# First four heads' rows stored and loaded ahead of the rest, in a two-layer transformer kernel on one Trainium2 core

## The chip, the cores and the metric

The program runs on one core of a Trainium2 chip. The core has five engines that run side by side and meet at semaphores: PE (TensorE, matmuls into PSUM), DVE (VectorE), ACT (ScalarE), POOL (GpSimd) and SP (SyncE), which here only issues DMAs. Sixteen DMA engines move the data. The metric is device time in microseconds, lower is better.

## The reference, cut to what matters

```python
# x is (4, 512, 128): B=4, T=512, C=128; H=16 heads of Dh=8
def _L0_attn_ref(x, W_qkv, b_qkv, W_out, b_out):
    qkv = (x @ W_qkv + b_qkv).reshape(B, T, 3, H, Dh).transpose(2, 0, 3, 1, 4)
    q, k, v = (qkv[0], qkv[1], qkv[2])
    ...
    q = q * cos + rotate_half(q) * sin
    k = k * cos + rotate_half(k) * sin
    attn = softmax(einsum('bhqd,bhkd->bhqk', q, k) / sqrt(Dh))
    out = einsum('bhqk,bhkd->bhqd', attn, v)
    return out.transpose(0, 2, 1, 3).reshape(B, T, C) @ W_out + b_out
...
x = _layernorm(x + _L0_attn_ref(x, ...))
x = _layernorm(x + _L0_ffn_ref(x, ...))      # 16 experts, top 4
x = _layernorm(x + _L1_attn_ref(x, ...))     # linear attention
x = _layernorm(x + _L1_ffn_ref(x, ...))      # linear layer with gated low-rank parts
```

## The kernel before

The kernel goes through the four batches of 512 tokens with everything resident in SBUF. The first 230 us are softmax attention of layer 0, and the rest is the expert layer and layer 1.

A head has only 8 dimensions, so one head's product q·k would use 8 of PE's 128 rows. Instead each float32 value is split into three bfloat16 parts (split_done0 counts the parts of k, split_done1 those of q), and all nine products of parts are summed in one bfloat16 matmul over 72 rows: 3 x 3 parts x 8 dimensions. These rows, the **stack**, are built by a trip through DRAM. `store_part` (L328) writes one part of one of the two, 128 rows of 512 tokens, three times over into `stack_dram[b, i]`, whose shape is 72 rows x 16 heads x 512 tokens (i is 0 for k and 1 for q). `load_stack` (L336) reads the 72 rows of four heads back, into `KS` or `QS`. `parts_st0` and `parts_st1` count the stores that landed, 16 for each DMA.

For each of 16 groups G (4 batches x 4 groups of four heads), PE first computes the scores only to find their row maxima (`scores_for_max`, L528; 16 matmuls for each group), and DVE reduces each to `negmax` (L1136). DVE then splits the 16 columns of maxima in parts (`split_max`, the CAST at L1145 is its first step, and `maxq_done` its end). PE transposes them (`max`, L663), ACT copies them to `maxp`, and SP writes them with `load_max` (L349) as three further rows of QS. Only then `scores` (L544) computes the transposed scores with the maximum already taken off, ACT takes the exponential (L837) and `values` (L553) multiplies with v. The maxima run 26 to 36 matmuls ahead of the exponentials.

At the start the order is written by hand. PE: 11 matmuls on zeros (`keep_warm`, L746), four rotary projections of batch 0 (L653), the values (L658), two projections of batch 1 (L653), 42 matmuls on zeros, and then the loop over the first 17 maxima with one matmul on zeros behind each. Behind it come 12 more on zeros, the transposition of the maxima, and nine more maxima, with the first four `scores` among them. DVE rotates batch 0 (L1268) and splits the third part; ACT splits the first two (L946). POOL sets zeros and then rotates and splits batch 1: k's half (seven operations) and q's half (seven operations), by `rope_split` and `rest_split`, and in `rope_split` it waits until the parts of batch 0 are stored, because it writes the same tile. SP issues all DMAs from one queue in program order, and a wait holds all that stand behind it.

Of the kernel before, what the change touches and what calls it, by code (L numbers as in the profile page):

```python
# [67 lines left out]
EARLY = dict(w_kq=4 * D, b_rope=4, cos=T, sin=T, w_v=D, ident=P, bv_row=D)  # L68
# [12 lines left out]

EARLY_AT, EARLY_N = columns(EARLY)
# [5 lines left out]
def program(nc, x_in, xT_in, early_in, late_in, identb_in, ones_in, stack_dram, w_dram, out):  # L88
    with ExitStack() as ctx:
# [9 lines left out]
        c_.update({k: late[:, a:b] for k, (a, b) in LATE_AT.items()})  # L99
        ident = c_["ident"]  # L100
# [67 lines left out]
        split_done = [sem(f"split_done{i}") for i in range(2)]  # L168
        parts_st = [sem(f"parts_st{i}") for i in range(2)]
# [151 lines left out]
        def _(sp):  # L321
            sp.dma_start(xT[:, 0:T], xT_in[:, 0:T]).then_inc(rope_ld, 16)
            for a, z_, done in (("w_kq", "w_kq", rope_ld), ("b_rope", "sin", table_ld), ("w_v", "bv_row", early_ld)):
                cols = slice(EARLY_AT[a][0], EARLY_AT[z_][1])
                sp.dma_start(early[:, cols], early_in[:, cols]).then_inc(done, 16)
            sp.dma_start(xT[:, T:2 * T], xT_in[:, T:2 * T]).then_inc(x_ld, 16)

# [7 lines left out]
            def load_stack(b, g, i):  # L335

                sp.wait_ge(parts_st[i], 48 * (b + 1))
                if b < 2 and g == 0:
                    if i:
                        sp.wait_ge(*((pad_pool, 3) if b else (pad_dve, 1)))  # L340
                    else:
                        sp.wait_ge(pad_pool, b + 1)
# [3 lines left out]
                sp.dma_start((KS, QS)[i][b % 2][0:SROW, h0:h1, :], stack_dram[b, i, :, h0:h1, :])\  # L346
                    .then_inc(qk_ld[b % 2][g], 16)
# [12 lines left out]
            def load_late(j):  # L360

                if j == 0:
                    sp.dma_start(late[:, 0:LATE_FIRST], late_in[:, 0:LATE_FIRST]).then_inc(late0_ld, 16)
                    return
                n = LATE_N - LATE_FIRST
# [61 lines left out]
        def _(pool):  # L427
# [95 lines left out]
        def _(pe):  # L523
# [871 lines left out]
```

## Time and profile before

| | us |
|---|---|
| median of 3 runs | 459.50 |
| lowest, highest | 459.38, 459.88 |
| profiled execution | 462.07 |
| its span, first to last instruction | 460.20 |

| engine | busy us | share of the span |
|---|---|---|
| PE | 427.8 | 93% |
| DVE | 368.2 | 80% |
| ACT | 241.1 | 52% |
| POOL | 104.1 | 23% |

Times of day below are in us from the start of the span. A row of the timeline names the start, the length, engine, line, operation, tile written and tile read, the shapes, the count, and in brackets how long the engine sat idle before it and on what. On the page, PEclk is the TensorE clock that was granted, as a share of 2.4 GHz: 0.50 is the lower of its two levels, 1.2 GHz.

### The profile page before, as it was taken

What the parts mean: (1) busy time and instruction counts of PE and PEld (TensorE: products, weight loads), DVE (VectorE), ACT (ScalarE), POOL (GpSimd) and SP (SyncE); (2) the same over time, 40 slices, a digit from 0 to 9 for tenths busy, and PEclk for the clock granted to TensorE, in tenths of its full rate; (3) what the DMA queues carried; (4) which work ended last, traced back from release to release, by engine and by line L of the source; (5) the groups of instructions that cost most, each with busy time, mean ns of one, the idle gap of its engine ahead of it and who ended that gap; (6) DMA issues with size and microseconds to landing.
All of it is one profiled execution on the core that took longest, in us unless ns stands there. A gap on an engine that the chain in (4) does not pass through costs nothing. (4 is left out here: it accounts for less than half of the span.)

```text
span 460.2 us, 7561 instructions
## 1 busy us (share of the span) xinstructions
PE 427.8 (93%) x2555; PEld 210.7 (46%) x2584; DVE 368.2 (80%) x1000; ACT 241.1 (52%) x452; POOL 104.1 (23%) x103
## 2 busy tenths in 40 slices
PE   8988989999899999999898999999999999998892
PEld 3333223223342334233232456665766675685671
DVE  6369988888798998999975298898886897887566
ACT  1502666876768776777578612236336623643320
POOL 9793052530528100200010000200120022003022
PEclk9979989999999999999999999999999999999997
DMA  4774524233351226331004122232031102000001
GB/s 143 257 192 145 156 59 113 61 104 89 84 164 35 84 76 153 116 121 32 18 7 94 25 69 90 82 80 70 24 91 48 47 32 82 25 1 24 1 1 47
DMA packets 24866, 36.16 MB, mean 79 GB/s; under 512 B 2678, under 2 KB 16246, under 8 KB 24822
## 3 DMA queue, kind: packets, MB, share of 16 engines
q1 hardware_dynamic: 24828, 35.67, 26.7%
q8 instruction: 21, 0.34, 0.3%
q14 instruction: 17, 0.14, 0.1%
HBM read 23.94 MB, written 11.53 MB: 77 GB/s over the span
## 5 line engine op out<-in xcount | busy, mean ns | idle before, releaser
L1136 DVE TENSOR_REDUCE negmax<-psum 128x1 f32<-128x512 f32 x256 | 163.5, 684 | 31.4 <-PE psum L536 31.0
L837 ACT ACTIVATE probs<-psum 128x512 f32<-128x512 f32 x256 | 137.4, 600 | 47.7 <-PE psum L551 40.5
L536 PE MATMUL psum<-KS,QS 125*128 125x512 bf16 x256 | 99.1, 390 | 8.1 <-DMA QS<-stack_dram 3.2
L551 PE MATMUL psum<-QS,KS 128*128 128x512 bf16 x234 | 88.0, 384 | 3.8 <-ACT probs L837 2.7
L566 PE MATMUL psum<-probs,VA 128*32 128x512 f32 x512 | 68.8, 609 | 0.3 <-ACT probs L837 0.3
L816 PE MATMUL psum<-xT,late 128*128 128x512 f32 x144 | 68.8, 600 | 0.0
L551 PEld LDWEIGHTS psum<-QS,KS 128*128 128x128 bf16 x256 | 24.6, 98 | 78.1 <-ACT probs L837 55.4
L458 POOL TENSOR_SCALAR var<-mv 128x4 f32<-128x4 f32 x16 | 3.6, 227 | 242.5 <-DVE mv L1043 242.4
L966 ACT ACTIVATE QS<-psum 128x512 f32<-128x512 f32 x36 | 21.6, 600 | 51.6 <-PE psum L816 51.6
L803 PEld LDWEIGHTS psum<-late,QS 128*128 128x128 f32 x288 | 35.7, 191 | 15.2 <-issue 10.2
L536 PEld LDWEIGHTS psum<-KS,QS 125*128 125x128 bf16 x256 | 25.4, 99 | 36.8 <-DVE negmax L1136 15.2
L1305 DVE SCALAR_TENSOR_TENSOR QS<-QS,psum 128x512 f32<-128x512 f32 x36 | 24.5, 680 | 20.7 <-ACT QS L966 20.5
L803 PE MATMUL psum<-late,QS 128*128 128x128 f32 x288 | 39.6, 280 | 0.3 <-DVE QS L1007 0.2
L749 PE MATMUL psum<-warm_in 128*128 128x512 bf16 x115 | 34.5, 418 | 1.6 <-POOL warm_in L490 1.5
L816 PEld LDWEIGHTS psum<-xT,late 128*128 128x128 f32 x144 | 24.6, 191 | 19.2 <-issue 18.0
L436 POOL TENSOR_TENSOR rot<-rot,early 128x512 f32<-128x512 f32 x12 | 15.3, 1272 | 73.8 <-ACT rot L859 71.3
L1007 DVE TENSOR_TENSOR QS<-QS,psum 128x512 f32<-128x512 f32 x32 | 21.8, 682 | 1.2
L1007 DVE TENSOR_TENSOR QS<-QS,cw 128x512 f32<-128x512 f32 x32 | 21.9, 686 | 0.4
L566 PEld LDWEIGHTS psum<-probs,VA 128*32 128x32 f32 x512 | 10.1, 108 | 23.7 <-ACT probs L837 18.2
L436 POOL TENSOR_TENSOR res<-res,late 128x512 f32<-128x512 f32 x12 | 13.8, 1150 | 30.8 <-ACT xT L878 30.8
L749 PEld LDWEIGHTS psum<-warm_in 128*128 128x128 bf16 x120 | 12.4, 106 | 17.0 <-issue 5.0
L878 ACT ACTIVATE xT<-psum 128x512 f32<-128x512 f32 x12 | 7.2, 599 | 22.9 <-PE psum L677 22.9
(146 smaller groups left out, 539.2 us busy)
## 6 DMA issues: line engine op xcount, KB each, us to landing
stack_dram<-parts SPq DMA_DIRECT2D x24, 384.0 KB, 3.4
cw<-w_dram SPq DMA_DIRECT2D x32, 256.0 KB, 3.2
KS<-stack_dram SPq DMA_DIRECT2D x16, 288.0 KB
QS<-stack_dram SPq DMA_DIRECT2D x16, 288.0 KB
late<-in_late SPq DMA_DIRECT2D x6, 330.5 KB, 4.6
res<-in_x SPq DMA_DIRECT2D x4, 256.0 KB, 5.8
w_dram<-wT SPq DMA_DIRECT2D x4, 256.0 KB, 4.3
out_y<-KS SPq DMA_DIRECT2D x4, 256.0 KB, 2.3
```

What stands on the lines that cost most here:

```text
L436: return nc.gpsimd.tensor_tensor(out=o, in0=a, in1=b, op=op)
L536: mm(sm_bank(u)[:, :], QS[b % 2][0:KROW, h, qt * P:(qt + 1) * P], KS[b % 2][0:KROW, h, :], start=True, stop=True).then_inc(sm_full, 1)
L551: mm(ps[v % 3][:, :], KS[b % 2][0:KROW + 3, h, kt * P:(kt + 1) * P], QS[b % 2][0:KROW + 3, h, :], start=True, stop=True).then_inc(s_full, 1)
L566: last_ = mm(ps[6][32 * j:32 * j + 32, :], VA[b % 2][:, kt, h, :], probs[:, n % 2, j, :], start=(kt == 0), stop=(kt == NT - 1), tile_posit ...
L749: mm(bank[:, :], warm_in[:, 0:P], warm_in[:, :], start=True, stop=True)
L803: last_ = mm(bank_of(u)[:, t * D:(t + 1) * D], hid[:, i % 3, t * P:(t + 1) * P], w2, start=(p == 0 and t == 0), stop=(p == EP and t == NT ...
L816: mm(bank_of(u)[:, :], wt, xT[:, b * T:(b + 1) * T], start=True, stop=True).then_inc(fullness(u), 1)
L837: fn(probs[:, n % 2, j, :], ps[v % 3][:, :], ACT.Exp, scale=float(DH) ** -0.5).then_inc(exp_done, 1)
L966: fn(gate_s[:, i % 2, :], bank_of(u)[:, :], ACT.Tanh, scale=0.5).then_inc(tanh_done, 1)
L1007: return V.tensor_tensor(out=o, in0=a, in1=b, op=op)
L1136: V.tensor_reduce(out=negmax[:, G % 4, i:i + 1], in_=sm_bank(u)[:, :], axis=X, op=ALU.max, negate=True).then_inc(sm_free, 1)
L1305: V.scalar_tensor_tensor(out=h_, in0=h_, scalar=1.0, in1=bank_of(g)[:, :], op0=ALU.add, op1=ALU.mult)\
```

## The change

For batch 0 alone, the heads lie in another order over the partitions: the first 32 partitions of q and k hold the first four heads. The weights, biases and tables for that order come in their own input, `in_begin`, which is loaded into columns of `late` that are not used until later. The tables for batches 1 to 3 are loaded behind the first inputs (`rest_ld`), and without the two weight blocks that these batches did not use.

The six stores of batch 0 become twelve: six of 32 partitions, and behind the loads of the first group six of 96 partitions. The first group is loaded in two halves of two heads each, and PE waits for the second half (`first_ld`) at its ninth score. The DRAM layout of batch 0's stack changes with it: 9 blocks of 128 rows, where a group is 32 rows next to each other. POOL waits for all of batch 0's stores as before, which are now twelve, and in front of q's half for `maxq_done` too. PE runs 38 matmuls on zeros instead of 42.

SP's queue before, from the stores of batch 0 to the stores of batch 1 (stack_dram is the stack in DRAM, KS0 and QS0 are k's and q's stacks of batch 0):

```order
L332 DMA stack_dram<-parts 128x3x512 [waits split_done0]
L332 DMA stack_dram<-parts 128x3x512 [waits split_done1]
L346 DMA KS0<-stack_dram 72x2048 [waits pad_pool,parts_st0]
L346 DMA QS0<-stack_dram 72x2048 [waits pad_dve,parts_st1]
L346 DMA KS0<-stack_dram 72x2048 [waits parts_st0]
L346 DMA QS0<-stack_dram 72x2048 [waits parts_st1]
L394 DMA xT<-in_xT 128x1024
L353 DMA QS0<-maxp 3x16x128 [waits maxp_done]
L332 DMA stack_dram<-parts 128x3x512 [waits split_done0] x3
```

The pair of stores stands there three times, and the pair of loads four times. SP's queue in the same place now:

```order
L366 DMA stack_dram<-parts 32x3x512 [waits split_done0]
L366 DMA stack_dram<-parts 32x3x512 [waits split_done1]
L375 DMA KS0<-stack_dram 72x1x1024 [waits pad_pool,parts_st0]
L375 DMA QS0<-stack_dram 72x1x1024 [waits pad_dve,parts_st1]
L366 DMA stack_dram<-parts 96x3x512 [waits split_done0] x3
L366 DMA stack_dram<-parts 96x3x512 [waits split_done1] x3
L356 DMA KS0<-stack_dram 72x1x2048 [waits parts_st0]
L356 DMA QS0<-stack_dram 72x1x2048 [waits parts_st1]
L430 DMA xT<-in_xT 128x1024
L381 DMA QS0<-maxp 3x16x128 [waits maxp_done]
```

The pair of small stores stands there three times, the pair of half loads twice, the pair of whole loads three times. The six larger stores have moved between the first group's loads and those of the other three groups, and all of them stand in front of the row of maxima.

POOL before, where it goes from k's half of batch 1 to q's half:

```order
L451 TENSOR_SCALAR parts<-rot 128x512 [waits pool_chain]
L436 TENSOR_TENSOR parts<-rot,parts 128x512 [waits split_done0]
L436 TENSOR_TENSOR rot<-rot,early 128x512 [waits parts_st1,rot_done]
L436 TENSOR_TENSOR rot<-rot,early 128x512 [waits pool_chain]
L436 TENSOR_TENSOR rot<-rot 128x512 [waits pool_chain]
```

and now:

```order
L487 TENSOR_SCALAR parts<-rot 128x512 [waits pool_chain]
L472 TENSOR_TENSOR parts<-rot,parts 128x512 [waits split_done0]
L472 TENSOR_TENSOR rot<-rot,early 128x512 [waits parts_st1,rot_done,maxq_done]
L472 TENSOR_TENSOR rot<-rot,early 128x512 [waits pool_chain]
L472 TENSOR_TENSOR rot<-rot 128x512 [waits pool_chain]
```

Nothing moved there; q's half waits for the split of the first maxima as well.

The diff, cut to its core:

```diff
+BEGIN = dict(w_kq0=4 * D, b_rope0=4, cos0=T, sin0=T)
-EARLY = dict(w_kq=4 * D, b_rope=4, cos=T, sin=T, w_v=D, ident=P, bv_row=D)
+EARLY = dict(w_v=D, ident=P, bv_row=D, w_kq=2 * D, b_rope=2, cos=T, sin=T)
...
+        begin = late[:, LATE_N - BEGIN_N:LATE_N]
...
+            sp.dma_start(begin[:, 0:n], begin_in[:, 0:n]).then_inc(rope_ld, 16)
+            sp.dma_start(begin[:, n:], begin_in[:, n:]).then_inc(table_ld, 16)
+            n = EARLY_AT["bv_row"][1]
+            sp.dma_start(early[:, 0:n], early_in[:, 0:n]).then_inc(early_ld, 16)
             sp.dma_start(xT[:, T:2 * T], xT_in[:, T:2 * T]).then_inc(x_ld, 16)
+            sp.dma_start(early[:, n:], early_in[:, n:]).then_inc(rest_ld, 16)
...
-                sp.wait_ge(parts_st[i], 48 * (b + 1))
+                sp.wait_ge(parts_st[i], 48 * (b + 2))
...
+                if b:
+                    src = stack_dram[b, i, :, h0:h1, :]
+                else:
+                    src = begin_stack(i)[:, HW * g:HW * (g + 1), :].rearrange("r (d k) t -> r d (k t)", k=HG)
+                sp.dma_start((KS, QS)[i][b % 2][0:SROW, h0:h1, :], src).then_inc(qk_ld[b % 2][g], 16)
+
+            def begin_stack(i):
+                return stack_dram[0, i].rearrange("(r d) h t -> r (d h) t", d=DH)
+
+            def begin_part(i, p, q0, q1):
+                sp.wait_ge(split_done[i], p + 1)
+                rows_ = begin_stack(i).rearrange("(x y) q t -> x y q t", x=3)
+                rows_ = rows_[p] if i == 0 else rows_[:, p]
+                sp.dma_start(rows_[:, q0:q1, :].rearrange("c q t -> q c t"),
+                             parts[q0:q1, i, p, :].unsqueeze(1).to_broadcast([q1 - q0, 3, T])).then_inc(parts_st[i], 16)
+
+            def begin_heads(i, h0, h1, done):
+                sp.wait_ge(parts_st[i], 48)
...
+                src = begin_stack(i)[:, 0:HW, :].rearrange("r (d k) t -> r d k t", k=HG)[:, :, h0:h1, :]
+                sp.dma_start((KS, QS)[i][0][0:SROW, h0:h1, :], src.rearrange("r d k t -> r d (k t)")).then_inc(done, 16)
...
             for p in range(3):
                 for i in range(2):
-                    store_part(0, i, p)
-            for g in range(NG):
+                    begin_part(i, p, 0, HW)
+            for h0, done in ((0, qk_ld[0][0]), (2, first_ld)):
+                for i in range(2):
+                    begin_heads(i, h0, h0 + 2, done)
+            for i in range(2):
+                for p in range(3):
+                    begin_part(i, p, HW, P)
+            for g in range(1, NG):
                 for i in range(2):
                     load_stack(0, g, i)
...
-                pool.wait_ge(parts_st[i], 48 * b)
+                pool.wait_ge(parts_st[i], 48 * (b + 1))
...
-            pool.wait_ge(table_ld, 16)
+            pool.wait_ge(rest_ld, 16)
             for i in range(2):
+                if i:
+                    pool.wait_ge(maxq_done, 1)
                 beside_pool("rope", 1, 2 * i)
                 beside_pool("split", 1, i)
...
+                if u == HG * NT // 2:
+                    pe.wait_ge(first_ld, 32)
...
-            keep_warm(42)
+            keep_warm(38)
```

## Rows read from the trace of the kernel before

**Rows 1.** Timeline of PE, 11 to 43 us

```profile
11.02 1.88 PE L653 MATMUL psum<-xT,early 128*128 128x512 f32 x4
12.74 9.23 PE L749 MATMUL psum<-warm_in 128*128 128x512 bf16 x41
25.12 0.59 PE L536 MATMUL psum<-KS,QS 125*128 125x512 bf16 x1 [3.16 <-DMA QS<-stack_dram]
...
35.34 0.38 PE L536 MATMUL psum<-KS,QS 125*128 125x512 bf16 x1 [0.16 <-DVE negmax L1136]
35.55 2.97 PE L749 MATMUL psum<-warm_in 128*128 128x512 bf16 x13
38.93 0.22 PE L663 MATMUL psum<-identb,maxq 128*48 128x128 bf16 x1 [0.40 <-issue]
...
42.03 0.38 PE L551 MATMUL psum<-QS,KS 128*128 128x512 bf16 x1 [1.04 <-DVE negmax L1136]
```

**Rows 2.** Table by stretch: us, busy of the engines, PEclk, DMA share, GB/s

```profile
22.00:25.12 3.12, 0.00 (x0) 0.03 (x1) 0.00 (x0) 0.00 (x0) 2.95 (x3) 0.87 0.68 193
25.12:31.10 5.98, 5.97 (x15) 2.06 (x16) 4.38 (x7) 0.00 (x0) 5.73 (x5) 0.50 0.84 214
31.10:37.00 5.90, 5.69 (x26) 2.47 (x26) 5.89 (x10) 0.00 (x0) 5.49 (x5) 1.00 0.46 110
```

**Rows 3.** Timeline of SP's queue: start and length of issues

```profile
1.18 1.36 SPq L325 DMA_DIRECT2D early<-in_early  x3
...
15.63 1.10 SPq L332 DMA_DIRECT2D stack_dram<-parts  x1
20.04 0.31 SPq L346 DMA_DIRECT2D QS<-stack_dram  x1
23.86 0.69 SPq L394 DMA_DIRECT2D xT<-in_xT  x1
39.48 0.92 SPq L353 DMA_DIRECT2D QS<-maxp  x1
```

**Rows 4.** Timeline of DVE, 13 to 51 us

```profile
13.44 1.47 DVE L1007 TENSOR_TENSOR parts<-rot,parts 128x512 bf16<-128x512 f32 x2
...
30.87 6.12 DVE L1136 TENSOR_REDUCE negmax<-psum 128x1 f32<-128x512 f32 x10 [0.16 <-PE psum L536]
37.02 1.18 DVE L1145 CAST maxq<-negmax 128x16 bf16<-128x16 f32 x1
...
50.87 0.17 DVE L1145 CAST maxq<-negmax 128x16 bf16<-128x16 f32 x1
```

**Rows 5.** Table by stretch, as in Rows 2: attention in full run

```profile
100.00:200.00 100.00, 97.05 (x556) 35.15 (x566) 87.97 (x195) 73.66 (x145) 23.25 (x20) 1.00 0.33 93
```

**Rows 6.** DMA issues: KB each, us from issue to landing

```profile
early<-in_early SPq DMA_DIRECT2D x1, 192.0 KB, 5.8
stack_dram<-parts SPq DMA_DIRECT2D x1, 384.0 KB, 2.5
...
stack_dram<-parts SPq DMA_DIRECT2D x1, 384.0 KB, 4.4
xT<-in_xT SPq DMA_DIRECT2D x1, 512.0 KB, 13.9
w_dram<-wT SPq DMA_DIRECT2D x4, 256.0 KB, 4.3
out_y<-KS SPq DMA_DIRECT2D x4, 256.0 KB, 2.3
```

**Rows 7.** DMA traffic of 16.5 to 19.5 and of 20 to 32 us

```profile
DMA packets 1034, 1.02 MB, mean 340 GB/s; under 512 B 38, under 2 KB 1034, under 8 KB 1034
...
DMA packets 677, 2.40 MB, mean 200 GB/s; under 512 B 93, under 2 KB 93, under 8 KB 676
q1 hardware_dynamic: 676, 2.39, 75.3%
```

**Rows 8.** Timeline of POOL, 19 to 38 us

```profile
19.05 2.61 POOL L436 TENSOR_TENSOR rot<-rot,early 128x512 f32<-128x512 f32 x2 [2.04 <-DMA stack_dram<-parts]
...
37.01 1.16 POOL L436 TENSOR_TENSOR parts<-rot,parts 128x512 bf16<-128x512 f32 x1
```

More of the change, by code:

```diff
@@ L79, in columns @@
     return out, at
+BEGIN_AT, BEGIN_N = columns(BEGIN)
 EARLY_AT, EARLY_N = columns(EARLY)
@@ L85, with program @@
 LATE_PIECES = 8
-def program(nc, x_in, xT_in, early_in, late_in, identb_in, ones_in, stack_dram, w_dram, out):
+def program(nc, x_in, xT_in, begin_in, early_in, late_in, identb_in, ones_in, stack_dram, w_dram, out):
     with ExitStack() as ctx:
@@ L99, in program @@
         c_.update({k: late[:, a:b] for k, (a, b) in LATE_AT.items()})
+        begin = late[:, LATE_N - BEGIN_N:LATE_N]
+        c_.update({k: begin[:, a:b] for k, (a, b) in BEGIN_AT.items()})
         ident = c_["ident"]
@@ L322, in _ @@
             sp.dma_start(xT[:, 0:T], xT_in[:, 0:T]).then_inc(rope_ld, 16)
-            for a, z_, done in (("w_kq", "w_kq", rope_ld), ("b_rope", "sin", table_ld), ("w_v", "bv_row", early_ld)):
-                cols = slice(EARLY_AT[a][0], EARLY_AT[z_][1])
-                sp.dma_start(early[:, cols], early_in[:, cols]).then_inc(done, 16)
+            n = 4 * D
+            sp.dma_start(begin[:, 0:n], begin_in[:, 0:n]).then_inc(rope_ld, 16)
+            sp.dma_start(begin[:, n:], begin_in[:, n:]).then_inc(table_ld, 16)
+            n = EARLY_AT["bv_row"][1]
+            sp.dma_start(early[:, 0:n], early_in[:, 0:n]).then_inc(early_ld, 16)
             sp.dma_start(xT[:, T:2 * T], xT_in[:, T:2 * T]).then_inc(x_ld, 16)
+            sp.dma_start(early[:, n:], early_in[:, n:]).then_inc(rest_ld, 16)
             def store_part(b, i, p):
@@ L335, in load_stack @@
             def load_stack(b, g, i):
-                sp.wait_ge(parts_st[i], 48 * (b + 1))
[L338 to L342, printed above, removed]
+                sp.wait_ge(parts_st[i], 48 * (b + 2))
+                if b == 1 and g == 0:
+                    sp.wait_ge(pad_pool, 3 if i else 2)
                 if b >= 2:
@@ L364, in load_late @@
                     return
+                if j == 1:
+                    sp.wait_ge(rot0_done, 4)
                 n = LATE_N - LATE_FIRST
@@ L652, in beside_pe @@
                         pe.wait_ge(x_ld, 16 * min(b, 2))
-                    last_ = mm(o[:, :], c_["w_kq"][:, m * D:(m + 1) * D], xT[:, b * T:(b + 1) * T], start=True, stop=True)
+                        pe.wait_ge(rest_ld, 16)
+                    w_ = c_["w_kq"][:, m // 2 * D:(m // 2 + 1) * D] if b else c_["w_kq0"][:, m * D:(m + 1) * D]
+                    last_ = mm(o[:, :], w_, xT[:, b * T:(b + 1) * T], start=True, stop=True)
                 if kind == "val":
@@ L1269, in _ @@
                     wait_full(dve, ("rope", 0, m))
-                    V.scalar_tensor_tensor(out=rot[:, m, :], in0=ps[m][:, :], scalar=c_["b_rope"][:, m:m + 1],
-                                           in1=c_["cos"] if m % 2 == 0 else c_["sin"],
+                    V.scalar_tensor_tensor(out=rot[:, m, :], in0=ps[m][:, :], scalar=c_["b_rope0"][:, m:m + 1],
+                                           in1=c_["cos0" if m % 2 == 0 else "sin0"],
                                            op0=ALU.add, op1=ALU.mult).then_inc(rot0_done, 1)
@@ L1352 @@
     sign = np.where(d < DH // 2, -1.0, 1.0)[:, None]
-    early = dict(w_kq=np.concatenate([wk[:, order], wk[:, partner], wq[:, order], wq[:, partner]], 1), w_v=wv,
-                 b_rope=np.stack([b_k[order], b_k[partner], b_q[order], b_q[partner]], 1),
-                 cos=np.cos(ang).astype(np.float32), sin=(np.sin(ang) * sign).astype(np.float32),
+    cos, sin = np.cos(ang).astype(np.float32), (np.sin(ang) * sign).astype(np.float32)
+    d0 = f % HW // HG
+    head0 = f // HW * HG + f % HG
+    order0, partner0 = head0 * DH + d0, head0 * DH + (d0 + DH // 2) % DH
+    begin = dict(w_kq0=np.concatenate([wk[:, order0], wk[:, partner0], wq[:, order0], wq[:, partner0]], 1),
+                 b_rope0=np.stack([b_k[order0], b_k[partner0], b_q[order0], b_q[partner0]], 1),
+                 cos0=cos[d0 * H], sin0=sin[d0 * H])
+    early = dict(w_kq=np.concatenate([wk[:, order], wq[:, order]], 1), w_v=wv, b_rope=np.stack([b_k[order], b_q[order]], 1),
+                 cos=cos, sin=sin,
                  ident=np.eye(P, dtype=np.float32), bv_row=rows(bq[2 * D:]))
@@ L1381 @@
         "in_x": np.ascontiguousarray(x), "in_xT": np.ascontiguousarray(x.T),
+        "in_begin": np.ascontiguousarray(np.concatenate([begin[k] for k in BEGIN], 1)),
         "in_early": np.ascontiguousarray(np.concatenate([early[k] for k in EARLY], 1)),
```

13 lines of the change are left out of this document (7 added, 6 removed).

## The prediction, made before the changed kernel was run

> **What bounds the kernel now.** I read the timeline of PE at the start first. PE has no data from 21.97 us on and starts the first maxima at 25.12, after 3.16 us idle on the DMA of QS [rows 1]. The table by stretch shows the price of that idle time: the granted clock is 0.50 from 25.12 to 31.10 and 1.00 again after it [rows 2]. SP's queue shows what the load waited for: the last store of the split parts was issued at 15.63 and the load of QS went out at 20.04, when it had landed [rows 3]. Its data were ready on DVE at 14.91 (13.44 + 1.47) [rows 4]. So 10.2 us pass between the last part and the first score: 5.1 us for the store and 5.1 us for the load. Behind the first score stands a chain that no engine shortens: 16 reductions, the split of the maxima (the CAST at 37.02) [rows 4], the transposition at 38.93 [rows 1], the row of maxima issued at 39.48 [rows 3], and the first transposed score at 42.03 [rows 1]. That matmul is my mark M. From there PE is 97% busy in the attention's full run [rows 5], in an order that the change leaves alone, so a shift of M reaches the end nearly whole. The number to forecast is M.
>
> **The change part by part.** *Inputs.* The load with the tables for later batches adds 1282 columns, 0.66 MB. Of the first inputs, three were issued from 1.18 to 2.54 [rows 3] and the last of these took 5.8 us [rows 6], so they are in by about 8.3. At 340 GB/s [rows 7] 0.66 MB more take 1.9 us, about 10.2. PE needs them for batch 1's projections, the second pair of the four matmul records from 11.02 on [rows 1]; 0.8 us of cover, and what is later than that is added to the end of the matmuls on zeros. I take 0.
>
> *Small stores.* A whole store of 384 KB with an empty queue lands in 2.5 us, the last of six in 4.4 [rows 6]. Moving 0.39 MB at 340 GB/s is 1.15 us, so 1.35 are fixed. A store of 96 KB is 0.3 us of data, 1.65 in all, if 32 partitions feed the engines as 128 do. The other bound is the nearest transfer from few partitions: 256 KB out of wT's 16 rows take 4.3 us against 2.3 for 256 KB out of 128 [rows 6]; a quarter of the bytes at that price gives 1.35 + 3/4 of a us = 2.1. I take 1.9, between them. The last one goes out at about 15.0 and lands at 16.9 instead of 20.04: 3.1 us.
>
> *Half loads.* Of the 5.1 us of a load, 1.4 are taken as fixed and 3.7 as moving the first pair, so a pair of half the size takes 1.85 to 2.5 us (the second if the rate falls to three quarters, below), and lands at 20.2 to 20.8. The matmuls on zeros are 38 instead of 42, 0.22 us each [rows 1], and end at 21.1. So PE starts at 21.1 without having been idle: 4.0 us earlier, and **at the full clock**. At half clock a score and its matmul on zeros took 0.85 us (5.98 us for seven of them [rows 2]); at the full clock DVE's 0.61 (6.12 over 10) [rows 4] sets the pace. The first reduction starts at 21.7, the thirteenth ends at 29.7 and the sixteenth at 31.5, against 37.0: 5.5 us. The second half of the load is needed at the ninth score, about 24.5, and lands at about 22 to 23.5, so it costs nothing.
>
> *The queue behind it.* This is where I expect half of the gain to go. Four half loads (0.59 MB), six larger stores (1.77 MB), six loads (1.77 MB) and xT (0.52 MB) now stand in a row from 17.9 on. Stores move at 340 GB/s and loads at 200 [rows 7]: 2.95 + 5.2 + 2.95 us bring group 1's pair in at 29.0, and 30.5 with 1.5 us of lag, as before the first pair had (its 0.59 MB need 2.95 us at that rate, and PE waited for 5.1). PE wants it for the 17th score at 29.7, so 0.8 us is lost there. From the 17th score to the transposition it is 3.6 us (35.34 to 38.93), of which 3.2 are the score and 13 matmuls on zeros [rows 1]: 30.5 + 3.2 = 33.7, and the row of maxima is issued at 34.3. It was issued at 39.48 into empty queues and needed 2.55 us. Now four loads (1.18 MB, 5.9 us) and xT are in front: 29.0 + 5.9 = 34.9, then xT. Before, xT landed at 37.8 (23.86 + 13.9) [rows 3, 6], and the eight loads took until 31.8 at that rate, so xT and the slowest DMA engine's lag took up to 6.0; without the lag xT is 1.5. The row of maxima therefore lands between 37 and 41. I take 39.7, near the upper middle, because it uses the same engines that served the loads. M is at about 39.9 instead of 42.03: **2.1 us** earlier.
>
> *GpSimd.* k's half of batch 1 started at 19.05 when k's stores had landed [rows 8]; they now land at about 24, and seven operations take 9.5 us, so it ends at 33.5, and q's half runs to 43 or 44. SP stands at q's stores until then; behind it are batch 1's loads and the next row of maxima, which went out at over 50 us before and is not held. The CAST took 1.18 us beside POOL's 1.16 us operation from 37.01 [rows 8], and 0.17 alone at 50.87 [rows 4]. POOL's first half now covers the time of the CAST, so some of it may stay. PE's matmuls on zeros end 0.4 us before the transposition anyway, so it is worth 0.4 at most; I count 0.
>
> **The sum.** 462.07 of the profiled execution - 2.1 = 460.0; it stands 2.6 us over the median of 459.5, so 457.4 is the forecast.
>
> **The rivals.** *A, the whole gain arrives.* The queues drain ahead of the row of maxima (landing at 37 to 37.5), and group 1 comes in time for the 17th score. Then M is 4 to 5.5 us earlier: 454.0 to 455.5. For it: the rate of 200 GB/s is a mean over a stretch of conflicts between engines, and the new layout reads a block of rows that lie together. Against it: in the old layout too the slowest of 16 engines lagged by several us.
>
> *B, the loads get slower and the row of maxima later than before.* In the old loads the DMA engines are 75% busy [rows 7], which is 12 of 16, and 12 divides their 72 rows. The new source is 9 blocks of 8 rows that don't follow on each other. If work is dealt to the engines by the outer count, 9 engines serve a load and the rate is 150 GB/s. Then group 1 is in at 17.9 + 3.9 + 5.2 + 3.9 = 30.9, with lag 32.4; PE has been idle for over 3 us, as it was before 25.12, and so runs its 13 matmuls on zeros at half the clock, 5.6 us instead of 2.8. The transposition is at 38.5, and the four loads and xT hold the queues until 40.3 to 44.8. M comes 0 to 3 us later, and another stretch at half clock can add 1 to 2: 459.5 to 463, with 461.5 as its middle. It decides the sign when the six loads run below about 160 GB/s. The Trainium skill states this rule (DMA: Bandwidth & Descriptors, "Why a DMA increments its semaphore by 16 and not by 1"): the number of DMA engines is the largest up to 16 that divides the slowest dimension of both sides, which makes 12 before and 9 now; the trace agrees for the 12, and nothing in it shows that an engine's own rate stays the same when fewer run.
>
> *C, nothing to measure.* The losses of the queue and the gain of the start cancel, or M moves by 2 us and the later attention gives it back (a gap and a spell of low clock that fall elsewhere): 458.6 to 460.4. *D, the start isn't earlier,* because the load's 5.1 us is fixed and not size: then the first score is at 22, 3 us earlier, with 1 us idle; that lies inside C and the forecast.
>
> **How the numbers follow.** Forecast (456.0 to 458.5) 0.35; A 0.18; B 0.27; C 0.20. Faster by over 0.2% (0.9 us, about what a measurement of this kernel can tell from no change) is the forecast and A: 0.53. Within it: 0.20. Slower: 0.27. The range leaves out the last part of A and of B: 454.3 to 462.0.
>
> **What would show it.** Right: first score at 21 to 22 with no idle time on PE in front and the clock at 1.00; the 16th reduction done near 31.5; PE waiting for the DMA of group 1 for 1 us or so at the 17th score; M near 40, waiting for the row of maxima, whose issue stands near 34.3. For A: M at 36.5 to 38. For B: the DMA share during the loads of batch 0 at 0.56 or less, a low clock behind the 17th score, M at 42 or later. Wrong altogether would be a first score after 23, or a gain at M that the end does not have.

## The result and the profile after

Four runs of each kernel on one chip gave a median of 463.89 us for the changed kernel (462.85 to 466.94) and 459.69 us for the kernel before (459.38 to 459.93): ratio 1.0113, 95% interval 1.0081 to 1.0145. **The change makes the kernel 1.1% slower**, and the time lies outside the range of 454.3 to 462.0. A later comparison on another chip (e10_after_again, below) gave 1.0092 (1.0059 to 1.0125).

The profiled execution took 462.85 us with a span of 461.1. This is PE's timeline at the start, which answers to [rows 1] (start, length, engine, line, operation, count, and in brackets the idle time before it and on what):

```profile
12.63 1.95 PE L696 MATMUL psum<-xT,early 128*128 128x512 f32 x4 [2.20 <-DMA early<-in_early]
14.42 8.36 PE L792 MATMUL psum<-warm_in 128*128 128x512 bf16 x38
22.62 0.38 PE L577 MATMUL psum<-KS,QS 125*128 125x512 bf16 x1
...
33.13 0.39 PE L577 MATMUL psum<-KS,QS 125*128 125x512 bf16 x1 [3.36 <-DMA QS<-stack_dram]
33.36 2.97 PE L792 MATMUL psum<-warm_in 128*128 128x512 bf16 x13
...
42.38 0.58 PE L592 MATMUL psum<-QS,KS 128*128 128x512 bf16 x1 [4.04 <-DMA QS<-maxp]
```

The first score no longer waits, as forecast. But PE now waits three times for a DMA: 2.20 us for the inputs of batch 1's projections, 3.36 us for group 1's stack at the 17th score, and 4.04 us for the row of maxima at the mark M. SP's queue, which answers to [rows 3], shows who stands in front:

```profile
10.09 4.69 SPq L366 DMA_DIRECT2D stack_dram<-parts  x6
...
16.86 0.75 SPq L375 DMA_DIRECT2D QS<-stack_dram  x1
...
19.23 5.42 SPq L366 DMA_DIRECT2D stack_dram<-parts  x6
...
28.15 0.74 SPq L356 DMA_DIRECT2D QS<-stack_dram  x1
...
32.04 0.47 SPq L430 DMA_DIRECT2D xT<-in_xT  x1
36.83 0.80 SPq L381 DMA_DIRECT2D QS<-maxp  x1
```

The six larger stores go out from 19.23 to 24.65, and q's part of group 1 only at 28.15, when the last of them has landed. The row of maxima is issued at 36.83 and in at 42.38: 5.55 us, against 2.55 for the same row before (39.48 to 42.03) [rows 1, 3]. Between 28.93 and 32.51 the other four loads and xT went into the queue, and they stand in front of it.

The table by stretch answers to [rows 2, 7] (length; busy us of PE, PEld, DVE, ACT, POOL; granted clock; DMA share; GB/s):

```profile
31.00:33.00 2.00, 0.00 (x0) 0.00 (x0) 1.93 (x5) 0.00 (x0) 1.91 (x2) 1.00 0.61 186
37.00:42.40 5.40, 1.36 (x8) 0.44 (x6) 2.34 (x4) 0.00 (x0) 5.14 (x4) 0.96 0.88 295
42.40:45.30 2.90, 2.90 (x7) 0.97 (x8) 1.28 (x2) 1.20 (x2) 1.33 (x2) 0.50 0.99 347
```

While loads of the new layout run (31 to 33; xT is issued behind them at 32.04), the DMA share is 0.61. The row of maxima waits in a stretch where the engines are 88% busy. Behind the wait of 4.04 us the granted clock is 0.50 for 2.9 us, which costs 1.45 by estimate: at the full clock the same matmuls would take half of the 2.9. The timeline of DVE, which answers to [rows 4]:

```profile
23.04 9.66 DVE L1180 TENSOR_REDUCE negmax<-psum 128x1 f32<-128x512 f32 x16 [8.22 <-PE psum L577]
32.73 0.17 DVE L1189 CAST maxq<-negmax 128x16 bf16<-128x16 f32 x1
```

The maxima run at DVE's pace (9.66 us for 16) and are done at 32.7, but their next link needs the 17th score, which comes at 33.13. The timeline of POOL, which answers to [rows 8], where its q half begins:

```profile
34.59 2.25 POOL L472 TENSOR_TENSOR rot<-rot,early 128x512 f32<-128x512 f32 x2
```

And the landings, which answer to [rows 6] (KB each, us from issue to landing):

```profile
stack_dram<-parts SPq DMA_DIRECT2D x6, 288.0 KB, 4.3
...
early<-in_early SPq DMA_DIRECT2D x1, 641.0 KB, 9.4
stack_dram<-parts SPq DMA_DIRECT2D x6, 96.0 KB, 1.9
...
xT<-in_xT SPq DMA_DIRECT2D x1, 512.0 KB, 10.0
```

### The profile page after: what moved, and what is told of

Its sections match the earlier page's. It is cut to its first block and busy times, and to the rows that moved or that the text cites. A ratio compares the mean times of both kernels' runs of the same rounds, so it can differ in the third digit from the quotient of the medians.

```text
span 461.1 us, 7592 instructions
## 1 busy us (share of the span) xinstructions
PE 426.6 (93%) x2580; PEld 209.3 (45%) x2580; DVE 367.0 (80%) x1000; ACT 241.6 (52%) x452; POOL 102.3 (22%) x103
## 3 DMA queue, kind: packets, MB, share of 16 engines
q1 hardware_dynamic: 25206, 36.33, 27.3%
## 5 line engine op out<-in xcount | busy, mean ns | idle before, releaser
L592 PE MATMUL psum<-QS,KS 128*128 128x512 bf16 x256 | 96.5, 385 | 6.7 <-DMA QS<-maxp 4.0
L577 PE MATMUL psum<-KS,QS 125*128 125x512 bf16 x256 | 97.3, 383 | 5.7 <-DMA QS<-stack_dram 3.4
L846 PEld LDWEIGHTS psum<-late,QS 128*128 128x128 f32 x288 | 35.7, 191 | 15.2 <-issue 10.2
L792 PE MATMUL psum<-warm_in 128*128 128x512 bf16 x116 | 32.7, 399 | 1.5 <-POOL warm_in L526 1.5
L472 POOL TENSOR_TENSOR rot<-rot,early 128x512 f32<-128x512 f32 x12 | 13.1, 1091 | 76.4 <-ACT rot L903 67.6
```

The lines of the kernel that those rows point to most:

```text
L472: return nc.gpsimd.tensor_tensor(out=o, in0=a, in1=b, op=op)
L577: mm(sm_bank(u)[:, :], QS[b % 2][0:KROW, h, qt * P:(qt + 1) * P], KS[b % 2][0:KROW, h, :], start=True, stop=True).then_inc(sm_full, 1)
L592: mm(ps[v % 3][:, :], KS[b % 2][0:KROW + 3, h, kt * P:(kt + 1) * P], QS[b % 2][0:KROW + 3, h, :], start=True, stop=True).then_inc(s_full, 1)
L792: mm(bank[:, :], warm_in[:, 0:P], warm_in[:, :], start=True, stop=True)
L846: last_ = mm(bank_of(u)[:, t * D:(t + 1) * D], hid[:, i % 3, t * P:(t + 1) * P], w2, start=(p == 0 and t == 0), stop=(p == EP and t == NT ...
```

## Experiments

In each, M is the start of the first transposed score, and the *marks* are the starts of the 16 transpositions of maxima, one for each group. From the fifteenth mark to the end it is 233.4 to 233.6 us in the profiles whose clock stays at 1.00 from 100 to 450 us, so a shift is settled at the marks. A *spell* is a stretch of some us at the low clock. The profiles of the runs are named by their labels, and before_again is e9_before_again.

### The kernel before, looked at again

> The kernel before, unchanged, for the spread of its runs and for a second profiled execution. Clock theory: its second profile either has the same spells at half clock (25 to 31 and 65 to 69) and a time near 462, or lacks one and is 1.5 to 3 us shorter. Rival: the same spells, the same profile, whatever the time of the runs beside it.

PE's timeline in this second profile, the same rows as [rows 1]:

```profile
24.04 0.38 PE L537 MATMUL psum<-KS,QS 125*128 125x512 bf16 x1 [2.57 <-DMA QS<-stack_dram]
...
32.46 0.38 PE L537 MATMUL psum<-KS,QS 125*128 125x512 bf16 x1 [1.28 <-DVE negmax L1137]
...
36.09 0.22 PE L664 MATMUL psum<-identb,maxq 128*48 128x128 bf16 x1 [0.44 <-issue]
39.17 0.38 PE L552 MATMUL psum<-QS,KS 128*128 128x512 bf16 x1 [1.02 <-DVE negmax L1137]
```

The table for the first scores:

```profile
24.00:31.00 7.00, 6.96 (x32) 2.98 (x32) 6.54 (x11) 0.00 (x0) 6.59 (x7) 1.00 0.83 212
```

This is the most important row of the study. The same program, with 0.6 us less of idle time in front of the first score (2.57 us against 3.16 [rows 1]), keeps the full clock here, where the execution of [rows 2] had 0.50 for 6 us. M is at 39.17, not 42.03, the marks are 36.09 and 48.95 instead of 38.93 and 51.81, and the span is 455.9 instead of 460.2 (the rest of the 4.3 is a second spell, at 65 to 70 us, which this profile lacks too). The medians say the same: 459.19 us here (12 runs, 457.29 to 462.0), and of the 35 runs of before on that chip 15 lie within 457.2 and 458.0, at a mean granted clock of 0.993 to 0.997, while the others, at 0.990 and below, take 458.3 to 462.8. So the forecast's base was an execution with two spells that many executions don't have. The Trainium skill (TensorE: Matmul & The Clock Gate, "What's actually happening") says that the monitor behind the clock observes PE on a beat of its own, free of the kernel's, so that the place of a change differs from run to run. The two profiles of one program differ by more than the place, since one has the spell and the other hasn't. The length of the gap doesn't decide it: the kernel of e7_pool, which is the kernel before with one more wait on POOL, ran at 0.50 behind 2.37 us of idle time at the same place.

Against this profile the loss of the changed kernel adds up: M 42.38 - 39.17 = 3.2; the second mark 53.62 - 48.95 = 4.7, which is that and the 1.45 of half clock; the fifth 91.94 - 86.81 = 5.1; the span 461.1 - 455.9 = 5.2. Of the 3.2 at M only 0.2 stand in front of the row's issue (36.83 against 36.64 in before_again), and 3.0 are its landing (5.55 us against 2.53). The gain of the early start is gone before that: the 17th score waits for group 1 until 33.13, where in before_again it waits for DVE until 32.46. This is a sum for one pair of profiles; the medians of the two kernels differ by 4.2 and 4.4 us.

### The changed kernel, looked at again

> The changed kernel unchanged, for its spread and a second look at its trace, as e9_before_again was for the kernel before. If the change itself puts the row of maxima late, the mark M (first transposed score) is again at 42 to 43 us, waiting for the DMA of QS from maxp, the 17th score waits again for the DMA of stack_dram until about 33, and the median is 462 to 465 (ratio 1.006 to 1.012). Rival: the 463.9 of the first comparison was as much a matter of where a stretch at granted clock 0.50 fell as the 459.5 of before; then M falls below 41 in this profile, or the median below 461.

Median 462.20 us (6 runs, 461.82 to 468.27), ratio 1.0092 (1.0059 to 1.0125) to a before of 457.79 on that chip. PE's timeline in its profile, and then the load of group 1's q rows in SP's queue:

```profile
35.10 0.61 PE L578 MATMUL psum<-KS,QS 125*128 125x512 bf16 x1 [6.21 <-DMA QS<-stack_dram]
35.50 5.71 PE L793 MATMUL psum<-warm_in 128*128 128x512 bf16 x13
...
44.18 0.38 PE L593 MATMUL psum<-QS,KS 128*128 128x512 bf16 x1 [0.95 <-DMA QS<-maxp]
```

```profile
30.11 0.75 SPq L357 DMA_DIRECT2D QS<-stack_dram  x1
```

Here q's load of group 1 went out at 30.11, 2 us later than in the first profile, the 17th score came at 35.10 and not at about 33, PE was idle for 6.21 us and the clock then low, and 13 matmuls on zeros took 5.71 us instead of 2.97. The row of maxima was issued so late (41.71) that the queue was empty again and it landed in 2.5 us. M is at 44.18, later than expected, by another division of the same loss: all of it lies in the wait for group 1 and its low clock, and none in the row's landing. The second mark (53.97) is only 0.35 us behind that of the first profile. The median lies in the range expected. (The profiled execution is the slowest of the six; 5.0 us of its excess are spells between 330 and 385 us.) In 10 runs of the changed kernel the lowest time is 461.8 and the highest mean clock 0.990; before, the lowest is 457.2 and the clock reaches 0.997. The slowdown is the change's, not an accident of the first comparison.

### Nine blocks alone

```diff
-stack_dram[b, i, :, h0:h1, :]      # 72 rows
+....rearrange("(r d) h t -> r d h t", r=9)[:, 0:DH, h0:h1, :]   # 9 blocks of 8 rows
```

This is the kernel before with batch 0's stack laid out so that its rows can't be merged to one dimension of 72.

> The kernel before, with one thing of the change alone: batch 0's stack lies in DRAM as 9 blocks of 8 rows with a gap behind each, so a load of 72 rows has an outer count of 9 as in the changed kernel. Stores, order and sizes stay. Queue theory (the changed kernel loses because the row of maxima and group 1 stand behind more bytes, not because the loads are slower): the DMA share during the loads falls from 0.75 to 0.56, but their rate only from 200 to about 175 GB/s, as the changed kernel's trace shows; the first score comes 0.3 to 1 us later than 25.12, the time is 0.2 to 1.5 us longer. Rival (the number of DMA engines is the cause): rate 150 GB/s, first score 1 to 1.5 us later, the time 2 to 4 us longer, most of what the changed kernel lost.

The timeline of SP's queue, of PE, and the table for 20 to 32 us:

```profile
20.10 0.76 SPq L350 DMA_DIRECT2D QS<-stack_dram  x1
```

```profile
25.83 0.59 PE L543 MATMUL psum<-KS,QS 125*128 125x512 bf16 x1 [3.78 <-DMA QS<-stack_dram]
```

```profile
20.00:32.00 12.00, 8.22 (x27) 2.97 (x26) 4.66 (x7) 0.00 (x0) 11.34 (x10) 0.72 0.58 165
```

The same table of the kernel before (second profile):

```profile
20.00:32.00 12.00, 8.62 (x39) 3.47 (x37) 7.54 (x13) 0.00 (x0) 11.36 (x9) 1.00 0.77 203
```

Median 460.71 us, ratio 1.0043 (1.0021 to 1.0065). That is 2.0 us, between the 0.2 to 1.5 of the one theory and the 2 to 4 of the other. Nine blocks cost: the DMA share falls from 0.77 to 0.58 and the rate from 203 to 165 GB/s, the issue of a load takes 0.74 to 0.95 us of SP instead of 0.31 to 0.37, and the first score comes 1.8 us later than in before_again (0.7 later than in the profile of before). A part of the 0.4% may be clock: behind the wait of 3.78 us the clock was low here too. Nine of 16 engines would be 0.56 and twelve 0.75, which is the rule of the Trainium skill (DMA: Bandwidth & Descriptors, "Why a DMA increments its semaphore by 16 and not by 1") that the prediction cited for rival B. Both rows agree with it. What doesn't hold is the rate of 150 GB/s that B worked out, with an engine's own rate the same in both: an engine moved 203 / (0.77 x 16) = 16.5 GB/s in the one and 165 / (0.58 x 16) = 17.8 in the other, and 186 / (0.61 x 16) = 19 in the changed kernel.

### Seventy-two rows in the changed kernel

```diff
-src = begin_stack(i)[:, HW * g:HW * (g + 1), :].rearrange("r (d k) t -> r d (k t)", k=HG)
+src = begin_stack(i)[g].rearrange("r (d k) t -> (r d) (k t)", k=HG)   # group outermost in DRAM
```

The larger stores become 18 of 32 partitions with it.

> The changed kernel with another layout of batch 0's stack in DRAM: each group's 72 rows lie one behind the other, so a load has an outer count of 72 again, and the six stores of 96 partitions become eighteen of 32. Queue theory: DMA share during loads 0.75, rate about 200 GB/s, group 1's pair lands 0 to 1 us earlier than 33.1, the row of maxima 1 to 2 us earlier; the time falls by 0.5 to 2 us. Rival (the number of DMA engines is the cause): the time falls by 3 to 4 us, to that of the kernel before or below.

SP's queue and PE's timeline:

```profile
16.23 0.31 SPq L376 DMA_DIRECT2D QS<-stack_dram  x1
...
17.40 8.54 SPq L367 DMA_DIRECT2D stack_dram<-parts  x18
```

```profile
12.82 3.48 PE L698 MATMUL psum<-xT,early 128*128 128x512 f32 x4 [2.43 <-DMA early<-in_early]
...
24.34 0.38 PE L579 MATMUL psum<-KS,QS 125*128 125x512 bf16 x1
...
32.77 0.38 PE L579 MATMUL psum<-KS,QS 125*128 125x512 bf16 x1 [1.28 <-DVE negmax L1182]
...
39.35 0.38 PE L594 MATMUL psum<-QS,KS 128*128 128x512 bf16 x1 [1.38 <-DMA QS<-maxp]
```

Median 461.89 us, ratio 1.0049 (1.0023 to 1.0075): about half of the loss is left. By the ratios the time fell by 2 to 3 us, between the 0.5 to 2 of the one theory and the 3 to 4 of the other. The issues are 0.31 us again, and the larger stores begin at 17.40 instead of 19.23. M is at 39.35, 3.0 us ahead of the changed kernel's and where before has it undisturbed; 2.65 of the 3.0 are the row's landing, 2.9 us (36.45 to 39.35) instead of 5.55. The 17th score no longer waits for a DMA, but this shows less than it seems: another spell, behind the wait for the inputs, put the first score at 24.34, so that DVE held the 17th until 32.77. Group 1 was in by then, 0.36 us before the changed kernel had it; how much sooner, the profile doesn't say. Its marks are 35.88, 49.12, 61.57 and 73.96, level with before_again's 36.09, 48.95, 61.76 and 74.14; the fifth is 87.42 against 86.81. At M the layout, with the small stores that come with it, was the largest part of the loss; e1_nine shows that the nine blocks by themselves cost 0.4% in the old kernel. What keeps the median at 461.89, with the marks level, is open. In the profile it is spells: from the fifteenth mark to the end it takes 236.8 us instead of 233.5, with low clock at 325 to 330 and 370 to 375 us.

### The row of maxima in front of the other loads

```diff
-for g in range(1, NG): load_stack(0, g, 0..1)
-xT; load_max(0)
+load_stack(0, 1, 0..1); load_max(0)
+for g in range(2, NG): load_stack(0, g, 0..1)
+xT
```

> The changed kernel with one move in SP's queue: the row of maxima of group 0 is issued in front of the loads of groups 2 and 3 and of xT. Queue theory: the first transposed score comes at 39 to 39.5 instead of 42.38, PE is idle before it for about 1 us instead of 4.04, no spell at half clock follows, and the time falls by 3 to 5 us, to 459 to 461. Rival (slow loads): group 1's pair, which PE waits for at 33.13, is not sooner, and the time falls by less than 1.5 us.

SP's queue and PE:

```profile
39.66 0.79 SPq L381 DMA_DIRECT2D QS<-maxp  x1
...
55.06 0.80 SPq L381 DMA_DIRECT2D QS<-maxp  x1
```

```profile
34.27 0.56 PE L579 MATMUL psum<-KS,QS 125*128 125x512 bf16 x1 [4.40 <-DMA QS<-stack_dram]
34.62 4.53 PE L794 MATMUL psum<-warm_in 128*128 128x512 bf16 x13
...
42.09 0.38 PE L594 MATMUL psum<-QS,KS 128*128 128x512 bf16 x1 [0.92 <-DMA QS<-maxp]
...
58.69 0.61 PE L594 MATMUL psum<-QS,KS 128*128 128x512 bf16 x1 [2.97 <-DMA QS<-maxp]
```

Median 466.37 us, ratio 1.0160 (1.0126 to 1.0194): worse than the change itself, where both theories expected a gain. The row now takes 42.09 - 39.66 = 2.4 us, as before in an empty queue: the 5.55 us of the changed kernel were the transfers in front of it. But this execution had a low clock behind the 17th score (13 matmuls on zeros in 4.53 us), and what was moved behind the row holds the next one: its transposition is at 51.87 and its issue at 55.06, since SP waited up to 3.0 us for stores of batch 1 to land, which stood behind the moved loads and xT. It then took 3.6 us to land, and PE is idle for 2.97 us at 58.69. One queue holds both; a wait that is taken from one row goes to the next.

### The idle gaps filled

e3_warm moves twelve of the matmuls on zeros into the 2.2 us wait for the inputs; e8_fill does that too and adds zeros in front of the 17th score and of M.

```diff
+            keep_warm(12)     # e3, e8: in front of batch 1's projections
-            keep_warm(38)
+            keep_warm(26)
+                if u == HG * NT: keep_warm(22)      # e8 alone
+                if u == START - 6: keep_warm(15)    # e8 alone
```

> The changed kernel with 12 of its 38 matmuls on zeros moved in front of batch 1's two projections, so that PE no longer stands for 2.2 us at 12.63 waiting for the tables of the later batches. Queue theory: the first score comes at 20.4 to 21.5 instead of 22.62 (this shows when the first pair lands), but the 17th still waits for group 1 at about 33 and the first transposed score still comes at about 42.4; the time is within 1 us of the changed kernel's. Rival (the late input is what was lost): everything moves up by 1.5 to 2 us.

> The changed kernel with matmuls on zeros in its three idle gaps: 12 of the 38 in front of batch 1's projections, 22 more in front of the 17th score and 15 more in front of the first transposed score. No transfer is changed. Clock theory: PE has no gap over 2 us before 43 us and no half clock, the first transposed score stays at 41 to 43, because the DMA queues hold it, and the time falls by 2 to 4 us, to 460 to 462. Queue theory alone (the spells cost nothing): the same time as the changed kernel within 1 us.

PE in e3_warm, then in e8_fill, and e8_fill's table for 20 to 60 us:

```profile
34.31 0.61 PE L577 MATMUL psum<-KS,QS 125*128 125x512 bf16 x1 [5.85 <-DMA QS<-stack_dram]
```

```profile
20.78 0.38 PE L577 MATMUL psum<-KS,QS 125*128 125x512 bf16 x1 [0.33 <-DMA QS<-stack_dram]
...
33.30 0.39 PE L577 MATMUL psum<-KS,QS 125*128 125x512 bf16 x1 [0.63 <-DMA QS<-stack_dram]
```

```profile
20.00:60.00 40.00, 38.98 (x185) 14.52 (x183) 31.41 (x55) 12.80 (x25) 17.45 (x14) 1.00 0.62 198
```

e3_warm: 462.56 us, ratio 1.0088 (1.0058 to 1.0118). e8_fill: 462.92 us, ratio 1.0083 (1.0052 to 1.0114). e3_warm is as expected; e8_fill misses the 460 to 462 of the clock theory. With the first scores of e8_fill 1.8 us earlier (20.78 instead of 22.62) the 17th still comes at 33.30, so an earlier start is worth nothing as long as group 1's load comes when it comes. With no gap left the clock stays at 1.00, and the second mark is 51.37 instead of 53.62; the lowest of 12 runs is 460.36 against 461.8. The medians of the two can't be told from that of the changed kernel. By the profile and the lowest run the spells are a part of the loss of about 1 to 2 us; the medians don't show it. The clock isn't all that varies here either: the four runs of e8_fill with a mean clock of 0.993 take 460.4 to 465.1 us, and the two runs of before on that chip with the same clock 457.4 and 457.8 us. The rest of the loss is then the queue's: e11_best below changes the queue and fills the gaps, and there the whole loss is gone.

### More zeros in the kernel before

```diff
-            keep_warm(42)
+            keep_warm(56)
```

> The kernel before with 56 matmuls on zeros instead of 42 in front of the first score, so that PE is never idle for 3.16 us there. Theory (a spell at half clock follows an idle gap of PE of some 3 us, not in every execution, and costs 1.5 to 3 us each): no half clock from 25 to 31, the first transposed score at 40 to 40.8 instead of 42.03 in the profile, and a median 0.5 to 1.5 us below the kernel before, less than the profile shows because the kernel before has the spell only in some of its runs. Rival (the clock there doesn't matter, since DVE sets the pace): the same time within 0.2%.

Its table for 60 to 70 us:

```profile
60.00:70.00 10.00, 8.40 (x37) 2.27 (x37) 8.31 (x14) 5.31 (x11) 8.06 (x7) 0.83 0.53 145
```

459.47 us, ratio 1.0007 (0.998 to 1.0034). There is no idle time in front of the first score and no low clock behind it, and M is at 39.19, as in before_again, but another one fell at 60 to 70. A median 0.5 to 1.5 us lower had been expected, and the interval leaves room for 0.9 at most: keeping PE busy in that one gap bought nothing to measure.

### GpSimd's wait alone

```diff
             for i in range(2):
+                if i:
+                    pool.wait_ge(maxq_done, 1)
                 beside_pool("rope", 1, 2 * i)
```

> The kernel before with one part of the change alone: POOL's q half of batch 1 waits for maxq_done too. The CAST of the first maxima then runs beside no operation of POOL: 0.17 to 0.3 us instead of 0.9 to 1.2. PE's matmuls on zeros cover most of that, so M moves by 0 to 0.4 us, and q's half ends at about 47 instead of 39 to 47, before anyone needs it: ratio 0.998 to 1.002. Rival: POOL's later end holds SP at batch 1's q stores when the second row of maxima (about 49) is ready, and M's gain is turned into a loss of 1 to 2 us at the second group.

DVE's timeline, the first step of the split:

```profile
35.35 0.17 DVE L1147 CAST maxq<-negmax 128x16 bf16<-128x16 f32 x1
```

458.39 us, ratio 0.9996 (0.9969 to 1.0022). The CAST takes 0.17 us instead of 1.18 [rows 4], and the marks are 36.78, 49.67, 62.48 and 74.86, no earlier than before_again's (this execution had a spell from 24.3 to 27.3 us, which before_again hadn't). In the changed kernel the wait holds nothing: POOL's q half starts at 34.59, when its k half ends, and the maxima were split at 33.6. This part of the change is neutral within 0.3%.

### All that was learned, in one kernel

e6_all has the stack of 72 rows, a semaphore for each group's stores, each group's load right behind its own stores, and the row of maxima in front of the last group's loads and xT. e11_best adds ten matmuls on zeros in front of the 17th score and moves three stores of batch 1 behind the second row of maxima.

```diff
+            begin_group(1)            # its six stores
+            begin_group(2)
+            load_stack(0, 1, 0..1)
+            begin_group(3)
+            load_stack(0, 2, 0..1)
+            load_max(0)
+            load_stack(0, 3, 0..1)
+            xT
```

> The changed kernel with everything that the trace asks for: a group's 72 rows one behind the other in DRAM (outer count 72 in the loads), stores by group, each group's loads waiting only for that group's stores, the row of maxima in front of group 3's loads and xT, 12 matmuls on zeros in front of batch 1's projections and 22 behind, and 5 more in front of the first transposed score. If queue and clock are the whole loss: first score at 20 to 21, 17th at 28 to 29 without waiting for a DMA, the row of maxima issued at about 32 and landed in 2.5 to 3 us, first transposed score at 34.5 to 37, and 453 to 457 us, faster than the kernel before. Rival (an early start is given back later, in the next rows or at the end): the first transposed score is early and the time still 458 us or more.

> e6_all with ten matmuls on zeros in front of the 17th score and with the three stores of batch 1's q parts moved behind the second row of maxima in SP's queue, so that SP no longer stands at them while that row is ready. If the early start was lost in e6_all to the half-clock stretch behind the 17th score (1.7 us) and to the held second row (2.3 us), then the 17th score comes at about 28.8 without the clock falling, the transposition at about 32, M at 34.5 to 35.5, the second row is issued within 0.7 us of its transposition (45 to 46), and the time is 453 to 457. Rival: what is gained in front of batch 0's attention is given back in the next groups, which wait for POOL, DVE or batch 1's stack in any case; then M is at 35 but the marks from group 2 on lie no more than 1 us ahead of e9_before_again's (61.8, 74.1, 86.8) and the time is 458 or more.

e6_all: 460.65 us, ratio 1.0034 (1.0004 to 1.0064), the time of its rival. Its 17th score came at 28.80 and M at 36.88, but the 13 matmuls on zeros behind the 17th took 4.66 us, and SP stood at batch 1's stores, which wait for POOL, when the second row of maxima was ready (its transposition was at 46.85):

```profile
36.44 12.14 SPq L342 DMA_DIRECT2D stack_dram<-parts  x6
...
49.18 0.74 SPq L383 DMA_DIRECT2D QS<-maxp  x1
```

e11_best: 457.83 us (12 runs, 455.76 to 460.47) against 457.79, ratio 0.9996 (0.9971 to 1.0020). PE's timeline, and the table of two stretches of its last part:

```profile
29.04 0.39 PE L593 MATMUL psum<-KS,QS 125*128 125x512 bf16 x1 [0.41 <-DMA QS<-stack_dram]
...
32.16 0.24 PE L722 MATMUL psum<-identb,maxq 128*48 128x128 bf16 x1
45.97 0.22 PE L722 MATMUL psum<-identb,maxq 128*48 128x128 bf16 x1 [1.00 <-DVE maxq L1072]
```

```profile
320.00:330.00 10.00, 10.00 (x54) 6.96 (x54) 7.17 (x21) 1.79 (x3) 1.26 (x2) 0.83 0.12 42
365.00:375.00 10.00, 10.00 (x48) 7.70 (x48) 8.11 (x31) 0.86 (x2) 2.51 (x4) 0.66 0.08 26
```

Here the early start does arrive: the first transposed score is at 35.26 (before_again 39.17), the fifth mark at 84.28 (86.81) and the fifteenth at 219.89 (222.42). Of the 3.9 us 0.95 are given back in the second group, where PE waits for DVE, whose second CAST took 1.01 us beside POOL, and 0.8 between the fourth mark and the fifth; 0.35 are won in between. The remaining 2.5 us don't show in the median, and in the profiled execution the end has them not either: from the fifteenth mark it is 238.5 us instead of 233.5, with two stretches of low clock in which PE was never idle. The lowest run is 455.76 against 457.41 of 23 runs of before. So its schedule is ahead by 2.5 us, and it is not shown to be faster: neither the 453 to 457 expected nor the 458 or more of its rival. What it does show, on the same chip as e10_after_again, is that layout, stores by group, the row's place, the filled gaps and the moved stores of batch 1 together take back the whole 0.9% that the change lost. Measured alone were only the layout (e4_group, half of it), the gaps (e8_fill, nothing in the median) and the row's place (e2_rowfirst, a further loss).

## Why the prediction was wrong

**Two steps failed: the base, and the wait for group 1.** The sum took M from 42.03 to 39.9 and called it a gain of 2.1. Undisturbed, M before is 39.17, so the forecast's own 39.9 was already a loss of 0.7. The text took "the granted clock is 0.50 from 25.12 to 31.10" for a property of the kernel that the change removes; it was a matter of the execution. That the profiled 462.07 us stood 2.6 over the median was seen and then subtracted as an offset, instead of being read as the price of spells that the fastest runs don't have. Without the spell of [rows 2] the row of maxima goes out at 36.64 before, not at 39.48, and most of the lead of the forecast's 34.3 is gone.

**The start came nearly as forecast.** Small stores landed in 1.9 us (1.9 taken) and the load of q's rows, which waits for them, went out at 16.86 (16.9 forecast). PE started at 22.62, without idle time and at full clock (21.1 forecast); the 1.5 us are the inputs, which came at 12.6 and not at 10.2. I had taken 0 for that with 0.8 of cover; the load of 641 KB landed 9.4 us after its issue. It cost nothing at M, since e3_warm and e8_fill started at 21 and got the 17th score no earlier. The 16 reductions ended at 32.7 (31.5). One bound of the small stores was mis-worked: 96 KB is three eighths of 256 KB and not a quarter, so its 2.1 should be 2.5; the 1.9 taken was right all the same.

**The wait for group 1 was mis-sized.** 0.8 us forecast, 3.36 measured: the pair was in at 33.1, not 30.5. The forecast let the pair follow the larger stores without a break, moving from 26.05 on. But SP waits until the whole set of them has landed (4.3 us each), and q's load was issued at 28.15: 2.1 us. From there it took 5.0 us instead of 4.45, in the nine-block form: 0.5 us. The new form has a part in the late issue too, which no term of the sum had: the four half loads took SP 0.73 to 0.94 us each, so that the larger stores began at 19.23, and at 17.40 in e4_group.

**The row of maxima fell where its queue put it.** Issued at 36.83 (34.3 forecast), it landed at 42.38 (39.7), outside the 37 to 41 allowed. Its own 5.55 us are close to the 5.4 that the forecast gave it; it was late because its issue was, by the 2.6 us of group 1. Against the kernel before, the 5.55 us are 3.0 over those in an empty queue; e2_rowfirst shows that they are the transfers in front, and e4_group that in the 72-row form 2.9 are left.

**The sum, closed.** The profiled 462.85 us are 5.45 over the forecast of 457.4, and four terms make 5.4 of them: 1.0 from the base (M at 39.9 put on before_again's 457.65 gives 458.4), 2.5 at M, 1.45 of low clock behind it, and 0.45 further on (0.8 less 0.35, below). That the queue would take a part of the gain was seen; with the right base the forecast's own M would already have been a small loss, and the late group 1, the low clock behind M and the 0.8 us further on made it about 1%.

**GpSimd** cost nothing, as counted, in the changed kernel and alone (e7_pool). From M on "a shift reaches the end nearly whole" held: 3.2 at M, 1.45 of low clock behind it, 0.8 between the fourth and fifth mark, less 0.35 in between, make 5.1 of the span's 5.2. The 0.8 was in no term: 13.47 us from the fourth mark to the fifth instead of 12.67, in every kernel of the changed family. POOL's two operations on the tables take 2.25 us there instead of 2.63, so that a later one falls on DVE's split of the maxima, whose second CAST takes 1.08 us instead of 0.16; this is read from the two timelines and was not tested.

**Rival B was right in kind** and got 0.27: loads at a share near nine of 16 (0.61, where its sign was 0.56 or less), PE idle for over 3 us at group 1, M at 42 or later. Its low clock behind the 17th score came in the second profile (e10_after_again) and not in the first. Its time, 461.5 with 463 as the end, was too low by 1 to 2 us, since it was summed from the same base. Which of the gaps brings the low clock differs from execution to execution: behind M in the one profile of the changed kernel, behind the 17th score in the other.

## What to carry to other kernels

Take the base of a sum from an execution whose clock row shows no spell, or from two profiles, and ask of every stretch of low clock whether the median holds it too. When a first group is brought forward in one DMA queue, write down what now stands in front of each later, small and urgent transfer (here a row of 12 KB), because the lead is lost there. The lead arrived at M only when every group's load followed its own stores and the row stood in front of all that wasn't yet needed. Keep the rows of a source mergeable into one long dimension.

## What the runs showed of the hardware

- A kernel with nearly the same gap runs on at full clock in one execution and at 0.50 in another: in front of the first score of the kernel before, full after 2.57 us idle (e9_before_again) and half after 3.16 (before) and 2.37 (e7_pool). Elsewhere it was half after 2.37 (e6_all, 17th score) and 2.43 (e4_group, inputs), full after 3.36 (17th score of the changed kernel), and half after 3.78, 4.04, 4.40, 5.85 and 6.21. A gap of 2.4 to 3.4 us is a risk and not a fixed price; where it is paid behind the 17th score, 13 matmuls on zeros take 4.5 to 5.7 us instead of 2.97.
- Stretches of low clock also fall where PE is busy without a break, at 320 to 335 and 365 to 385 us, in three of the thirteen profiles (e4_group, e10_after_again, e11_best), and cost 3.3 us in e4_group and 5 us in the other two. No run here says what brings them.
- A load whose source has nine outer blocks takes SP 0.73 to 0.95 us to issue. One of 72 rows takes 0.31 to 0.37 us, but more behind a full queue: the last two of eight took 0.74 and 1.01 us in the kernel before. From the issue of the first of the eight loads to that of xT it was 6.6 us in e1_nine, and 5.0 and 4.5 us in the two profiles of before.
